# Both halves of the down product side by side on TensorE, behind the slot of score loads that stood between them

## The reference, cut to what matters

```python
# attention: 16 heads of 16, each query sees its own block of 32 keys and the 3 best earlier ones
sel = top4(gate(q, mean of k over each block)); mask = sel_of_token & causal
p = softmax(where(mask, q @ k.T * d ** -0.5, -1e30)); o = p @ v
o = o * rsqrt(mean(o * o) + eps) * o_norm_w;          s = o @ Wo.T
# feed-forward: 8 experts (width 176, weighted by comb: two of the router's 8 scores), and a shared one (352)
g = silu(x @ w_gate) * (x @ w_up)
g_out = (g * comb) @ w_down + (silu(x @ sw_gate) * (x @ sw_up)) @ sw_down
```

## Time and profile before

| | |
|---|---|
| median of 3 runs | 426.93 us (424.57 to 427.4) |
| span of the profiled execution, first to last instruction | 422.4 us |
| TensorE matmuls busy | 348.9 us, 83% of the span |
| VectorE busy | 300.3 us, 71% |
| GpSimd, ScalarE busy | 172.9 us and 170.7 us, 41% and 40% |
| layer 0 up to the end of its preparation | 0 to 96 us of the span |
| first pass, second pass | 96 to 190 us, 190 to 297 us |
| rest of layer 0, layer 1 | to 319 us, to 422.4 us |

### The profile page before, as it was taken

How to read it: one execution, slowest core, us unless ns; L and a number is a source line. 1 busy time by engine, 2 the same in 40 slices (tenths; PEclk the granted TensorE clock), 3 DMA queues, 4 the chain that set the end, 5 groups by cost and what they waited for, 6 DMA issues and landing times. The chain is left out here.

```text
span 422.4 us, 6057 instructions
## 1 busy us (share of the span) xinstructions
PE 348.9 (83%) x2028; PEld 240.3 (57%) x2028; DVE 300.3 (71%) x857; ACT 170.7 (40%) x305; POOL 172.9 (41%) x119
## 2 busy tenths in 40 slices
PE   0697767668779989999999999999682888996881
PEld 0586555546546657676665665656581776444641
DVE  3867489867997877894444764684668859758794
ACT  1422453551224323226444445544212475956610
POOL 5654283473444642554256526664536000000023
PEclk9999689697999999999999999999966789999898
DMA  8300168987793311212211141110006100000011
GB/s 267 74 23 21 50 160 178 163 141 182 183 180 88 87 47 44 70 37 52 63 43 42 40 137 39 39 37 2 1 2 216 48 0 2 0 1 0 2 50 50
DMA packets 17009, 30.20 MB, mean 71 GB/s; under 512 B 3140, under 2 KB 12012, under 8 KB 16556
## 3 DMA queue, kind: packets, MB, share of 16 engines
q1 hardware_dynamic: 12946, 18.80, 19.2%
q10 hardware_dynamic: 4032, 11.01, 9.0%
HBM read 24.99 MB, written 4.82 MB: 71 GB/s over the span
## 5 line engine op out<-in xcount | busy, mean ns | idle before, releaser
L388 POOL TENSOR_TENSOR wl<-wr,wh 128x768 fp32r<-128x768 f32 x28 | 51.2, 1829 | 65.3 <-ACT wh L474 49.1
L530 ACT ACTIVATE PT<-bank 128x512 f32<-128x512 f32 (+1 forms) x88 | 44.3, 557 | 39.5 <-PE bank L952 39.4
L687 DVE TENSOR_REDUCE mx<-bank 128x1 f32<-128x384 f32 (+3 forms) x88 | 52.2, 635 | 7.2 <-PE bank L934 6.9
L149 PE MATMUL bank<-xh,wh 128*128 128x512 f32 x112 | 50.7, 452 | 4.0 <-DVE gb L812 1.4
L426 POOL TENSOR_TENSOR gl<-gb,gh 128x512 fp32r<-128x512 f32 x28 | 36.5, 1302 | 37.5 <-DVE gh L819 24.9
L151 PE MATMUL bank<-xh,wl 128*128 128x512 f32 x112 | 45.7, 408 | 0.0
L150 PE MATMUL bank<-xl,wh 128*128 128x512 f32 x112 | 45.5, 407 | 0.0
L933 PE MATMUL bank<-KS,QS 112*128 112x128 bf16 (+3 forms) x128 | 32.9, 310 | 12.5 <-DVE mx L687 6.8
L1213 POOL TENSOR_TENSOR left<-xn,x 128x256 f32<-128x256 f32 x8 | 7.0, 898 | 85.1 <-DVE xn L1440 85.1
L149 PE MATMUL bank<-wh,gh 128*128 128x256 f32 x112 | 36.9, 329 | 0.5 <-POOL gl L426 0.5
L537 ACT ACTIVATE th<-bank 128x512 f32<-128x512 f32 x28 | 16.7, 597 | 45.9 <-PE bank L151 45.8
(11 more groups left out here) (233 smaller groups left out, 824.7 us busy)
## 6 DMA issues: line engine op xcount, KB each, us to landing
wr<-in_w_chunks_dram ACTq DMA_DIRECT2D x28, 384.0 KB, 3.1
KS<-parts_dram SPq DMA_DIRECT2D x12, 256.0 KB, 8.0
parts_dram<-wp SPq DMA_DIRECT2D x12, 128.0 KB
QS<-parts_dram SPq DMA_DIRECT2D x2, 768.0 KB
parts_dram<-x SPq DMA_DIRECT2D x12, 128.0 KB
w_ai<-in_w_ai_dram SPq DMA_DIRECT2D x1, 1152.0 KB, 6.6
x<-in_x_dram SPq DMA_DIRECT2D x2, 512.0 KB, 6.6
QS<-parts_dram SPq DMA_DIRECT2D x2, 512.0 KB
```

The source lines that it names most:

```text
L149: pe.matmul(out, l_hi, r_hi, start=start, stop=False, skip_group_check=skip)
L388: pool.tensor_tensor(wl[:, s % 3, :, :], wr[:, s % 2, :, :], wh[:, s % 3, :, :].bitcast(F32), ALU.subtract).then_inc(wl_ready, 1)
L530: act.activation(PT[:, k % 8, 0:n], bank[k % 2][:, 0:n], ACT.Exp, scale=float(DH) ** -0.5).then_inc(P_ready, 1)
L687: dve.tensor_reduce(mx[:, b * TB + i, heads[0]:heads[-1] + 1], bank[k % 2][:, 0:len(heads) * n].rearrange("p (h n) -> p h n", n=n), AX.X, ...
```

## The change

The slot of score loads, `slot(s * SLOTS + 2)`, which stood between the two halves of the down product in TensorE's program, moves in front of the first half. It does so in all steps from 1 to 27. No instruction is added or removed, and the programs of the other engines and their waits stay as they are.

```diff
                 up_product(s)
                 slot(s * SLOTS + 1)
+                slot(s * SLOTS + 2)
                 if s >= 1:
                     down(s - 1, 0)
-                slot(s * SLOTS + 2)
-                if s >= 1:
                     down(s - 1, 1)
                 slot(s * SLOTS + 3)
```

## The result

| | before | changed |
|---|---|---|
| median | 426.75 us (424.57 to 427.4, 4 runs) | 437.09 us (435.05 to 439.04, 4 runs) |
| span of the profiled execution | 422.4 us | 433.1 us |
| its mean granted clock | 0.935 | 0.933 |

The changed kernel takes 1.0274 times as long, 95% interval 1.023 to 1.0319: 10.3 us slower, where 10.4 were forecast.

What follows compares the result with a forecast made beforehand. From step 8 on TensorE's program was taken to bound the kernel, VectorE setting the pace in steps 5 to 7. First pass 6.2 plus second pass 4.2 made 10.4 us, added to 426.93: 437.3 us, range 432.5 to 440.5 (8 in 10).

Steps and rivals of the forecast that it cites:

- steps 1 to 4: Ahead of the first score load: the moved half lands in the wait for the bias rows' DMA, 0 us.
- steps 5 to 7: First pass, VectorE selecting blocks: only the later gate product and its tanh show, 0.3 us each, 0.9 us together.
- The price of a half: Read in step 12: the second down half delays load e by 0.8 us, some of it the change of kind.
- steps 9 to 15: First pass: load e comes 0.8 us later in steps 9 and 11 to 15, 4.8 us; step 10 gives 0.
- Step 8: First pass: 0.8 us for the half, less 0.1 for earlier d and 0.2 for f's wait, 0.5 us.
- step 10: First pass: load e already waits 1.77 us for VectorE's parts of the maxima, covering the second half, 0 us.
- steps 20 and 24: Second pass: slot 2's transposes wait for VectorE's copy, so the half comes behind: 0.8 and 0.65 us, 1.45 together.
- steps 16, 18, 22 and 23: Second pass, no sum over values in slot 1: c and d wait for exponentials, mean 0.65 us each, 2.6 us.
- The clock: New waits inside the passes last 0.3 to 1.3 us and lose no clock; 0 us taken.
- Not slower: Rival: VectorE sets the first pass's pace and covers the second half, 425.3 to 427.8 us; chance 0.07, faster by over 1% 0.03.
- Every step pays: Rival: the covers fail and all 22 steps pay 0.8 us, 17.6 us, giving 444.5 us; chance 0.09.
- Only the first pass pays: Rival: exponentials release banks quicker or the second pass has slack, 433.1 us, down to 432; chance 0.15.

Runs made afterwards that it cites:

- The third bank: Score loads go round three banks instead of two: old order, steps 11 to 15 423.78 us, whole first pass 421.35 us; changed order, steps 11 to 15 432.35 us.
- filler: Changed kernel plus six unread gate-product matmuls into bank 2, between slot 1 and slot 2 in steps 5 to 7: 432.61 us, ratio 1.0178 to the kernel before.
- changed, again: The changed kernel run once more without any edit, against the kernel before: 437.96 us, ratio 1.0288.
- three banks, new order: Changed kernel with three score-load banks in the whole first pass, except around the two transposes into bank 2: 432.69 us, ratio 1.0171 to the kernel before.
- the pair ahead of slot 2: Kernel before with both down halves together in front of slot 2, nothing between slot 2 and slot 3: 430.52 us, ratio 1.0118.

## Why the prediction was right, and where it wasn't

**Direction and total.** +10.3 measured (+12.2 the second time), +10.4 forecast. The parts tried alone add up to it: 2.9 + 3.8 + 3.8 and about 0 for steps 1 to 4 make 10.5 (9.2 with that part's -1.3). That the total was met so closely is luck: in the profile the first pass grew by 8.9 us (4.6 + 4.3) and not by 6.2, the second by 3.4 and not by 4.2, and 1.67 us came from ahead of the first load. The 2.9 us of steps 5 to 7 are the softest part, since by its ratio that kernel is no slower (1.0024, 0.9989 to 1.0059). Layer 1 kept its length, as forecast: from the tanh of step 27 to the end it is 126.34 us before and 126.48 in the changed kernel.

**Two banks couple the engines; the halves hid the reading.** Shown by the traces, step by step: the waits appear where they were placed, d starts when b is read and no earlier, e comes one half later, and the steps in which other work covers the reading pay nothing for the same pair. The third bank confirms that the banks hold the loads back (0.3 to 0.6 us a step in either order), but it isn't a cure for the new order: set against the old order with three banks, the pair still costs 3.05 us in steps 11 to 15.

**The price of a half.** 0.8 was read from one gap that held a change of kind. At the marks it is 0.68 to 0.73. That is the 4.3 instead of 4.8 in steps 9 to 15.

**Step 8 and step 10.** Step 8 gave 0.53 in the kernel where only steps 8 to 15 moved, for 0.5. Step 10 gave 0.02, covered by a wait on VectorE, for 0.

**The second pass by steps.** The steps that pay and those that don't are the forecast ones, steps 20 and 24 with their transposes among them: 0.71 and 0.57 for 0.8 and 0.65. For steps 16, 18, 22 and 23 the prediction took 0.65 as the mean of 0.8, 0.5, 0.65 and 0.8, which is 0.69, so its own steps add up to 2.75 us and not 2.6; they measured 2.5. The timeline of the changed kernel shows the transposes of step 20, answering to the earlier trace rows, and of step 23, the neighbour of the step in the earlier trace rows, ScalarE waiting for a load and load c for ScalarE:

```profile
242.42 0.66 PE L985 MATMUL bank<-ident,oT 128*128 128x128 f32 x4 [0.61 <-DVE oT L707]
...
270.83 1.57 ACT L530 ACTIVATE PT<-bank 128x512 f32<-128x512 f32 x3 [1.64 <-PE bank L952]
...
271.48 0.10 PEld L951 LDWEIGHTS bank<-QS,KS 115*128 115x128 bf16 x1 [0.75 <-ACT PT L530]
```

The waits of line 951 came to 7.5 us, of which 3.6 fall in steps 16, 18, 22 and 23, for which 2 to 4 were forecast. The rest was not foreseen, and most of it costs nothing. In step 19 the row of load c says 0.84 us of waiting for ScalarE, but the weight load behind the sum over values stood idle for the same 0.84 us before the change, put down to no wait, while the sum's matmuls ran; the step got 0.11 us shorter. So the waits of a line and its cost are not one number. Only the marks price a step.

**The clock: the step that failed.** "New waits inside the passes last 0.3 to 1.3 us", and so no loss. In the changed kernel that holds from step 8 on. In steps 5 to 7, load c waits for a VectorE that is selecting blocks, and it waited already, with a half of 0.7 us (and its own loads behind it) in front of the wait. I asked there only what the end of the step would pay, found 0.3 us, and didn't ask how long TensorE would now stand still: 2.8 to 3.3 us. In the profiled run the lower clock made about 3.9 of the 4.6 us, an estimate (43.60 less the 39.69 with filler, where the wait is 1.5 us and the clock 1.00). The reason given for no loss doesn't hold either: the 1.77 us of step 10 left the clock at 1.00 in the one execution that was read, but in two other kernels with the old order a wait of 1.76 us there had a fall behind it. Also missed was the pause before the first load: 1.64 us in the changed kernel where 4.0 were expected, because the clock had been at 0.50 from 88 to 91 us, in the steps ahead of it; the wait for the DMA hid that.

The Trainium skill, page TensorE: Matmul & The Clock Gate, section HAM oscillation — how this bites in real kernels, tells of a kernel in which waits between bursts of matmuls lower the clock, and each burst pays for it again. The trace agrees in kind, with three falls in 33 us, but not every such wait has one: 2.68 and 2.76 us left the clock at 1.00 with steps 5 to 7 changed alone. The section that the prediction named, Loop structure matters more than you think, was read there as speaking for the new order, since matmuls of a kind follow each other. The measurement decides otherwise: grouping products leaves a bare wait elsewhere, and the waits are what the clock went by.

**The rivals.** Not slower, and VectorE as the pace of the first pass, fell with the idle time of 1.21 us in step 12. Its condition was also put too low. Slower reductions would make d wait longer for b, so the backlog behind d is two reductions less d's 0.2 us; to reach 1.6 us they would have to take some 0.9 us, not 0.7. Every step pays fell with steps 10, 17, 19, 21, 25 and 26. Only the first pass pays fell with the +3.8 us of steps 16 to 27. The rule behind the rival of all steps, of the section Identifying Performance Opportunities of the Trainium skill's Perfetto Trace Analysis, holds where the reading isn't covered: there the repeated gap did mean too few banks, and a third shortened it (to 12.4 us of waits from 17.4 in the kernel before, ratio 0.991).

**What was also forecast.** The first load was to stay at 96.2 us. It came at 94.54, but by what happened ahead of the change, and at 96.04 where only steps 1 to 4 moved; with that the forecast of 0 for them stands. Of the gain of up to 2 us from fewer changes of kind at most 0.4 showed: steps 19, 21, 25 and 26 of the second pass gained 0.09 to 0.11 each. That it comes from the changes of kind is argued, not tested.

## What to carry to other kernels

Work that stands between two loads into a pair of buffers isn't a delay of the second load: it hides the reader's time, so price such a move by what each load will then wait for, step by step, and look first for the steps where something else covers it. In steps where another engine sets the pace, ask a second question, how long TensorE will stand still at a stretch, since its clock may then cost more than the order does, in some executions and not in others. And when a remedy is tried on the changed kernel, try it on the old one too: the third bank seemed to cure the new order until it was set beside the old order with the same bank. Where loads wait for their reader in many steps, try one more buffer before another order: here it was worth 4.4 us, and none of the orders tried gained any.

## What the runs showed of the hardware beyond that

No length of wait decided by itself whether TensorE's granted clock fell. Waits of score loads for VectorE in steps 5 to 10, over all fourteen profiles:

| wait | clock fell to 0.50 | clock stayed at 1.00 |
|---|---|---|
| 2.7 to 3.3 us | 2.79, 3.00, 3.26 (changed); 2.68, 3.26 (changed, again); 2.75, 2.76 (three banks in steps 11 to 15, new order) | 3.00 (the same kernel); 2.68, 2.76 (only steps 5 to 7); 2.67, 2.69 (three banks, new order) |
| 2.12 us | step 10 with the pair ahead of slot 2 | |
| 1.4 to 1.9 us | 1.76 in step 10, twice (only steps 1 to 4; three banks in steps 11 to 15, old order) | 21 others |

The two waits of 3.00 us, both in step 6, went both ways. This is the one behind which the clock held, with three banks in steps 11 to 15 in the new order:

```profile
111.66 0.10 PEld L950 LDWEIGHTS bank<-KS,QS 112*128 112x128 bf16 x1 [3.00 <-DVE mx L702]
...
113.00:115.00 2.00, 2.00 (x17) 1.00 0.35 121
```

The falls began between 0.6 us before the end of the wait and 1.8 us behind it, most of them with TensorE at full work again, so a row at 0.50 can have its cause in the rows ahead of it. What decides between the two outcomes was not found.

Six matmuls whose result nobody reads, in three steps, made the changed kernel some 4 us faster (1.0178 against 1.0274), and did nothing for the kernel whose waits were shorter, 0.2 to 1.6 us in those steps (1.0019).
